# Moving the carry clip of a selective-scan kernel from GpSimd to VectorE, with two changes of order in the second pass

## The reference, cut to what matters

```python
xn = layernorm(x)
x_and_res = xn @ in_proj_w.T + in_proj_b          # 1024 -> 2048
x_in, res = silu(x_and_res[..., :1024]), x_and_res[..., 1024:]
ssm = x_in @ x_proj_w.T + x_proj_b                # 16 (delta) + 1024 (B) + 1024 (C)
delta = clip(softplus(dlt_raw @ dt_proj_w.T + dt_proj_b), 1e-5, 0.1)
A = clip(-exp(A_log), -5, -0.01)                  # 1024 x 16
def step(h, (dt, Bt, Ct, xt)):                    # over 2048 time steps
    dA = clip(exp(A * dt[..., None]), 1e-6, 1)
    h  = clip(h * dA + (Bt * dt * xt)[..., None], -100, 100)
    y  = sum(h, -1) * Ct + D_param * xt
y * silu(res) @ out_proj_w.T + out_proj_b         # + x + a 1024 -> 1024 "ffn" of xn
```

## Time and profile before

| | us |
|---|---|
| median of 2 runs | 2274.73 (2273.91 to 2275.55) |
| profiled execution, its own time | 2279.52 |
| its span, core 0 (the slowest of 8) | 2278.0 |
| spans of the other cores | 2253.9 to 2270.1 |
| busy in the span: DVE, ACT, PE, POOL | 1493.0, 1265.8, 1243.7, 745.8 |

### The profile page before, as it was taken

The page is one execution under the profiler, slowest core; times in us unless marked ns, Lnnn a source line. Parts: engine busy times, 40 slices in busy tenths (PEclk is TensorE's granted clock), DMA queues, the critical chain, the costliest instruction groups (busy, mean ns, idle before and its releaser), DMA issues.

```text
span 2278.0 us, 22411 instructions; the slowest of 8 cores (2253.9 to 2278.0 us)
## 1 busy us (share of the span) xinstructions
PE 1243.7 (55%) x5104; PEld 512.8 (23%) x5104; DVE 1493.0 (66%) x1344; ACT 1265.8 (56%) x2001; POOL 745.8 (33%) x826
## 2 busy tenths in 40 slices
PE   1221846147472957196728771776278536755444
PEld 1111312012031413042313220322133212322012
DVE  2332033067993989388948894789578966988980
ACT  0004464277556955596558655875578447845531
POOL 0000041316233272327232723262326342543221
PEclk9999966578575968597758775887588767877557
DMA  5672322611002400231033103220322022302001
GB/s 141 190 181 66 112 70 40 53 43 55 1 28 83 126 24 21 91 111 39 10 102 92 57 1 111 83 67 1 111 71 79 0 84 79 93 6 74 0 10 65
DMA packets 106888, 151.98 MB, mean 67 GB/s; under 512 B 53232, under 2 KB 53240, under 8 KB 106760
## 3 DMA queue, kind: packets, MB, share of 16 engines
q1 hardware_dynamic: 97128, 120.10, 17.9%
q0 software_dynamic: 6176, 19.93, 4.2%
q10 hardware_dynamic: 3456, 10.52, 1.5%
HBM read 124.26 MB, written 26.25 MB: 66 GB/s over the span
## 4 chain that ended last, share of the span: by engine, by line
PE 37%; DVE 15%; issue 15%; ACT 12%; DMA 10%; POOL 9%; SPq 1%; DVEq 1%; ACTq 0%; POOLq 0%
DVE h_buf L853 13%; PE pM L703 7%; PE pS L578 6%; DMA xr_t<-x 6%; PE pM L668 5%; PE pO L606 5%; PE pO L611 4%; PE pO L668 4%; ACT da L903 3%; POOL out_tm L494 2%; PE pO L703 2%; POOL wf L405 1%; PE pT L540 1%; ACT xnf L1006 1%; DMA x_t<-w_x 1%
## 5 line engine op out<-in xcount | busy, mean ns | idle before, releaser
L853 DVE TENSOR_TENSOR_SCAN h_buf<-da,cr,Bu 128x512 f16<-128x512 f16 x768 | 1019.0, 1395 | 264.8 <-PE pS L578 200.4
L903 ACT ACTIVATE da<-dlt,ac 128x512 f16<-128x512 f16 x1024 | 686.1, 714 | 219.2 <-DVE h_buf L853 218.6
L578 PE MATMUL pS<-h_buf,eye 128*128 128x512 f16 x1024 | 422.8, 478 | 325.4 <-DVE h_buf L853 252.8
L853 DVE TENSOR_TENSOR_SCAN h_buf<-da,Bu 128x512 f16<-128x512 f16 x256 | 322.5, 1326 | 283.8 <-ACT da L903 127.1
L440 POOL TENSOR_SCALAR cr<-h_buf 128x4 f16<-128x4 f16 x256 | 157.7, 618 | 737.9 <-DVE h_buf L853 735.6
L578 PEld LDWEIGHTS pS<-h_buf,eye 128*128 128x128 f16 x1024 | 108.6, 107 | 562.0 <-issue 499.6
L703 PE MATMUL pM<-xin,rx 128*128 128x512 f16 (+1 forms) x832 | 198.2, 383 | 27.3 <-ACT sres L1038 23.4
L475 POOL TENSOR_TENSOR Bu<-y_s,sres 128x512 f16<-128x512 f32 x64 | 120.6, 1885 | 70.2 <-DVE y_s L833 70.2
L668 PE MATMUL pM<-xnf,rin 128*128 128x512 f16 x512 | 134.3, 411 | 3.9 <-ACT sres L1038 2.5
L606 PE MATMUL pO<-Bu,wo 128*128 128x512 f16 x512 | 133.5, 408 | 3.2 <-POOL Bu L475 3.2
L450 POOL TENSOR_TENSOR mcol<-mcol,sumx 128x1 f32<-128x1 f32 x32 | 18.0, 561 | 356.3 <-ACT xin L970 356.3
(11 more groups left out here) (89 smaller groups left out, 1561.8 us busy)
## 6 DMA issues: line engine op xcount, KB each, us to landing
rin<-wt_in SPq DMA_DIRECT2D x128, 256.0 KB, 2.8
rx<-wt_x SPq DMA_DIRECT2D x128, 256.0 KB, 2.7
x_t<-x SPq DMA_DIRECT2D x32, 512.0 KB, 4.6
xr_t<-x POOLq DMA_DIRECT2D x32, 512.0 KB, 4.6
y<-out_tm SPq DMA_DIRECT2D x32, 512.0 KB, 2.9
wt_in<-rin SPq DMA_DIRECT2D x16, 256.0 KB, 2.8
wt_x<-rin SPq DMA_DIRECT2D x16, 224.0 KB, 3.8
x_t<-w_in ACTq DMA_DIRECT2D x4, 512.0 KB, 4.0
```

The lines of the kernel that those rows point to most:

```text
L578: TCH(te.matmul(sbank[:, :], eye16[:, :], h_sl(gn), start=(n == 0), stop=(n == NST - 1)))
L853: VCH(v.tensor_tensor_scan(h_sl(gn), da_r[gn % DAR][:, :], Bu[P][k][:, :], init, op0=ALU.mult, op1=ALU.add))
L903: ACH(sc.activation(da_r[gn % DAR][:, :], dlt[Ps][k][:, :], AF.Exp, scale=c_(a_cols[k], n)))
```

## The change

Three edits:

1. The clip leaves POOL's list and becomes a DVE instruction behind every fourth scan. It reads what the scan just ahead of it wrote, so it waits on DVE's own semaphore for that scan (`vsw(s_n)`). The waits of scans for POOL's clips go; what takes their place is a wait on DVE's own counter (`vsw(cn)`, `vsw(last_clip)`), which by then has always been passed.
2. In pass 1 ACT calls `apump` in the in-projection as in the other passes: da's in groups, then four evacuations in a row.
3. Due times in POOL's list of pass 1: "w4" 18.5 in place of 22.0, "attn" of tiles 0 and 1 at 23.4 and 44.2 in place of 44.0 both.

```diff
                 if w == 1:
-                    ev.append((22.0, "w4", 0))
+                    ev.append((18.5, "w4", 0))
...
                     for k in range(DCH):
-                        rd_a = (16 * k + 18) * SCAN_NS
-                        if cS == 0 and k < 2:
-                            rd_a = 44.0
-                        ev.append((rd_a, "attn", k))
-                    for jl in range(32):
-                        ev.append(((4 * jl - 4) * SCAN_NS, "clip", jl))
+                        ev.append(((16 * k + 18) * SCAN_NS, "attn", k))
...
                 for _rd, kind, idx in ev:
-                    if kind == "clip":
-                        jl = idx
-                        gn_c = 4 * jl + 3
-                        k_c, n_c = gn_c // NST, gn_c % NST
-                        wt(gp, "v", ("scan", cS * 128 + gn_c))
...
-                        GCH(gp.tensor_scalar(
-                            carry[k_c][:, n_c - 3:n_c + 1], src_ap,
-                            100.0, -100.0, op0=ALU.min, op1=ALU.max))
-                        mark(("pclip", cS * 32 + jl), GCH)
...
                             wt(v, "t", ("summ", G - HR))
-                            if (G - HR) % 4 == 0:
-                                wt(v, "g", ("pclip", (G - HR) // 4))
-                        if gn == 0 and cS >= 1:
-                            wt(v, "g", ("pclip", cS * 32 - 1))
+                            cn = clip_n.get((G - HR) // 4, 0)
+                            if cn > 0:
+                                vsw(cn)
+                        if gn == 0 and last_clip[0] > 0:
+                            vsw(last_clip[0])
                         init = 0.0 if ci == 0 else c_(carry[k], n)
-                        VCH(v.tensor_tensor_scan(
+                        s_n = VCH(v.tensor_tensor_scan(
                             h_sl(gn), da_r[gn % DAR][:, :], Bu[P][k][:, :],
                             init, op0=ALU.mult, op1=ALU.add))
                         mark(("scan", G), VCH)
+                        if n % 4 == 3:
+                            vsw(s_n)
+                            base = (gn - 3) % HR
+                            src = bass.AP(h_buf, base * TC + TC - 1,
+                                          [[HR * TC, 128], [TC, 4]])
+                            clip_n[(cS * 128 + gn - 3) // 4] = VCH(
+                                v.tensor_scalar(carry[k][:, n - 3:n + 1], src,
+                                                100.0, -100.0, op0=ALU.min,
+                                                op1=ALU.max))
...
                     for m in range(16):
-                        if cP == 1:
-                            apump()
-                        elif m % 4 == 0:
+                        if m % 4 == 0:
                             apump(block=True)
```

More of the change, by code:

```diff
@@ L431, in _ @@
                 for _rd, kind, idx in ev:
-                    if kind == "clip":
-                        jl = idx
-                        gn_c = 4 * jl + 3
-                        k_c, n_c = gn_c // NST, gn_c % NST
-                        wt(gp, "v", ("scan", cS * 128 + gn_c))
-                        base = (gn_c - 3) % HR
-                        src_ap = bass.AP(h_buf, base * TC + TC - 1,
-                                         [[HR * TC, 128], [TC, 4]])
-                        GCH(gp.tensor_scalar(
-                            carry[k_c][:, n_c - 3:n_c + 1], src_ap,
-                            100.0, -100.0, op0=ALU.min, op1=ALU.max))
-                        mark(("pclip", cS * 32 + jl), GCH)
-                    elif kind == "w4":
+                    if kind == "w4":
                         emit_w4()
@@ L815, in _ @@
             mark(("bcomb",), VCH)
+            clip_n = {}
+            last_clip = [0]
             ep2_n = [0]
@@ L870, in _ @@
                 emit_epi(cS, DCH - 1, P)
+                last_clip[0] = clip_n.get((cS * 128 + 124) // 4, 0)
         @blk.scalar
```

## The result

The changed kernel takes 2263.6 us (median of 19 runs) against 2278.1 (18 runs). The ratio is 0.9931 [0.9915, 0.9946]: 0.7% faster, where I had forecast 1.8%. By the bound of 2% it is no change.

The account below looks back on a forecast made before the run. No engine is full; DVE is the nearest bound, the rest waiting. Pass 1 -25.2, passes 2 to 7 -15.8, pass 8 +0.9 make -40.1 from 2279.5, less 4.8 for the median: 2235 us predicted, range 2203 to 2273.

Parts of the forecast that it names:

- The price of a clip: On DVE, each clip moves the next scan by 0.265 us, taken as 0.28, between 0.08 and 0.6.
- rival (a): On DVE, the clip is nearly free: all 120 at 0.08 us, giving 2211 us; chance 0.17.
- The number of clips that count: Clips on the path that sets the end: 17 in pass 1, 14 per middle pass, 19 in pass 8; 120, 33.6 us.
- The 2.0 us are hidden, with 0.5 left: Middle passes: seven clips up to scan 27 delay scan 29 by 2.0 us, but PE's output transposes start later still.
- those between 29 and 70 fall into DVE's waits: Middle passes: clips behind scans 29 to 70 cost nothing, falling into DVE's waits for PE's sums and ACT's da's.
- The residual adds: Passes 2 to 8: first add 2.25 us earlier, a 1.09 us clip between adds gone; -3.25 a pass, bounds 0 and -4.
- The dfin events: Late in passes: DVE's 9.8 us of clip waits go, POOL collisions take 6.5 back; net -3.3 a pass, -1.5 to -5.5.
- rival (d): Pass ends: slower, DVE's clip queues behind POOL; decides from 0.61 us a clip, 2321 us at 1.0; chance 0.05.
- Pass 1: Scattered loads and in-projection: -27 from the stop and table loads, -3 from late events, plus 17 clips at 0.28: -25.2 us.
- This end stays: Pass 1: the last scattered load still ends at 460.64 us, so scan 40 starts at 462.7, 10.9 us earlier.
- Rival (c): Pass 1 gains only DVE's own shift, PE and ACT bounding it behind the stop: -11, not -27; 2251 us; chance 0.1.
- Pass 8: Last scan pass: -3.25 from the adds, -1.2 from a clip wait, plus 19 clips at 0.28: +0.9 us.

Follow-up runs that it names:

- e4: The changed kernel with each clip behind the second scan after the one it reads, so its wait is long past: 2226.55 us, ratio 0.9767 against before.
- e9: The changed kernel without clips (carried state left out), plus the bare wait for the scan just issued behind every fourth scan: 2248.66 us, ratio 0.9842 against before.
- e3: The changed kernel without any clip instruction, carry set to zero once, so the carried state is left out: 2212.65 us, ratio 0.9708 against before.
- e1: The kernel before with only ACT's new order in pass 1 (da's in groups), clips still on POOL: ratio 0.9945 against before.
- e2: The changed kernel with ACT's order of pass 1 put back as before, clips on DVE and new due times kept: ratio 0.9957 against before.
- e5: The changed kernel with each clip one scan later, one scan between the scan it reads and the clip: 2219.86 us, ratio 0.9736 against before.

## Why the prediction was too good

**The price of a clip** is the step that failed first: "0.11 + 0.155 - 0.08 = 0.185 behind it: 0.265 us, and a little". The 0.11 and the length (0.17) were right. The "- 0.08" was taken from the epilogue, where the instruction behind L833 has been prepared while L833 runs. Behind a clip it hasn't: DVE has stood at the wait until the scan ended, the clip is over in 0.17, and the scan's own waits come only after the clip has been sent. The trace's records of semaphore instructions (they stand in none of the views) have two of them 0.07 apart between the clip at 2120.23 and the scan at 2120.40; in e4 they come behind the scan that follows a clip. In e9 three of them stand in a row behind a scan that ends at 2104.55: the wait for it at 2104.60, the next scan's own two at 2104.66 and 2104.73, and the scan starts at 2104.80. Where only one stands behind the end, ahead of L833 and ahead of a clip, the gap is 0.10 to 0.11; with three it is 0.24. So a bare wait is worth 0.11 + 0.08 = 0.19 us, and the scan's two semaphore instructions, otherwise executed while the scan ahead runs, make it 0.32. That these set the gap is my reading of the records; no run took them away. The Trainium skill (VectorE: DVE Perf Modes, "The DRAIN you can't avoid") says, from a measurement of eight copies, that a semaphore between two DVE operations costs nothing extra. That would have been rival (a), 2211 us; e9 measures 0.32 us for it, and here the measurement decides.

**The number of clips that count.** In middle passes I counted 14. By the table (after less without clips) a pass pays 6.3 us, of which 4.3 belong to the 13 clips behind scans 75 to 123, 0.33 each. The other 2.0 fall where I had 0.3: 0.9 up to scan 42 and 1.0 between 42 and 72. There the steps "The 2.0 us are hidden, with 0.5 left" and "those between 29 and 70 fall into DVE's waits" failed. The seven clips to scan 27 made DVE 2.5 us late at scan 28 (after against e3), not 2.0, which used up the cover; my own line on what happens without that cover (each further 0.1 us a clip costs 0.7) was the right warning. A wait for PE's sum also hides a clip only if PE doesn't wait for the scan behind the clip in its turn, as it does in pass 4 (0.80 us at 1107.66).

In all, clips cost 6.2 + 6 x 6.3 + 9.1 = 53 us by the table, where I had 33.6. This term of the sum is what the forecast failed on. Some 10 of the 20 too few are these clips of the middle passes; the others are the price, and pass 8 (9.1 against 5.3), where scans set the pace nearly throughout.

**The residual adds**, -3.25 a pass: the mechanism was right (the load is no longer late, the add follows ACT) and the size wrong: -1.8 without clips, -0.9 with them. The bound of 0 to -4 held. I had read both parts from one pass of one core. There the first add started 2.3 us behind the end of ACT's evacuation; on the mean of the cores and middle passes it was 1.7, and it is 0.3 now: 1.5 gained, not 2.25. With the clips the evacuation itself ends 0.9 later in the pass (0.2 without), which takes back part of it. From the first add to the second it is 0.3 to 0.5 us less, not 1.0, since the next load sets it.

**The dfin events**, -3.3 a pass: -4.0 without clips. This term was right, and a little low. DVE's clips do collide there, which I had not priced. Their cost in this stretch, 2.3 us a pass for seven, is the usual 0.33 each, but most of it is not the wait, as it is elsewhere: e9's bare waits cost 0.6 there. DVE in the dfin events of the pass that starts at 1070.3:

```profile
1275.62 0.87 DVE L849 TENSOR_SCALAR cr<-h_buf 128x4 f16<-128x4 f16 x1
1276.40 7.25 DVE L839 TENSOR_TENSOR_SCAN h_buf<-da,cr,Bu 128x512 f16<-128x512 f16 x4
```

and POOL at that time:

```profile
1274.40 2.07 POOL L499 TENSOR_TENSOR Bu<-Bu,xin 128x512 f16<-128x512 f16 x1
1276.43 1.15 POOL L504 TENSOR_TENSOR Bu<-Bu,xin 128x512 f16<-128x512 f16 x1
```

The clip waits until POOL's product ends, 0.87 in place of 0.17. The product behind such a clip takes 1.15, so the products are not nearly all at 2.06 as forecast. This is rival (d)'s place, at the events only, and it never reached its deciding point of 0.61 us a clip on average: the 13 late clips cost 0.33 each.

**Pass 1**: -25.2 forecast, -23.3 measured, as -29.5 plus 6.2 of clips. The step "This end stays" failed: the last load ends 3.3 us later in the pass, and scan 40 with it. Why the loads end later wasn't tried. That the whole came out within 2 us is luck in part, since what is behind scan 55 was better than forecast by 1.8. Rival (c) (-11) is out, though e1 and e2 show that its opposite, two parts that add up, wasn't right either.

**Pass 8**: +0.9 forecast, +6.6 measured; without clips -2.5, where I had -4.4. Of the 5.7 missed 3.8 are the clips and 1.9 the gain; which part of the gain stayed out isn't shown.

So of the 26 us missed in passes 1 to 8 (-40 against -14), 19 are the clips' cost and 7 the gains. Of my three signs of being wrong one was met, that a middle pass grows: it grew by 0.5. The two fifths of the forecast that I gave to times under 2229 didn't follow from its own range either, of which 2 us of 19 lie there.

## What to carry to other kernels

Don't let an in-order engine wait for its own last instruction: it loses not the wait alone but its lead. Here that was 0.32 of a small instruction's 0.36 us in an undisturbed row, and two thirds of what 256 of them cost. If the data allow, put one other instruction between; the same work then cost 0.05 in such a row, and 11 us in place of 53 in all. Before counting such costs as hidden, give each cover its remainder in us and price the step again at the upper end of the unknown: a cover with 0.5 left is none.

## What the runs showed of the hardware

- A wait of DVE for the instruction directly ahead costs 0.32 us by itself where two more semaphore instructions follow it (e9), and 0.19 where none does (L833 in the earlier trace rows). Semaphore instructions of DVE that stand in a row come 0.07 apart. With one scan of 1.2 us between the two nothing of the wait is seen (e5). The lists of waits have 0.5 us of it in the changed kernel; only the gaps in the timeline show it.
- A small DVE instruction behind a running scan starts 0.08 ahead of its end, lasts 0.14 and moves the next by 0.05 (e4, e5).
- Beside a POOL instruction on 128x512 the same clip lasts 0.87, or about 1.05 when it doesn't wait for its scan (e5, pass 8, beside an attn that starts at 2123.43 and takes 1.70):

```profile
2124.10 1.06 DVE L832 TENSOR_SCALAR cr<-h_buf 128x4 f16<-128x4 f16 x1
```

  On core 0, 30 clips of the changed kernel last over 0.7, 64 in e5 and 25 in e4. Yet e5 isn't slower than e4: 1.1 us a middle pass against 1.5. Why these collisions cost so little wasn't tried.
